# Cosine attention: the four transfers of the inverse norms divided between SyncE and ScalarE

## The reference

```python
def _L1_attn_ref(x, w_q, w_kv, w_out, b_out, scale):
    ...
    q = _l2norm(q) * jnp.exp(scale)
    k = _l2norm(k)
    sim = jnp.einsum('bhid,bhjd->bhij', q, k)
    attn = jax.nn.softmax(sim, axis=-1)
    out = jnp.einsum('bhij,bhjd->bhid', attn, v)
    out = out.transpose(0, 2, 1, 3).reshape(b, s, h * out.shape[-1])
    return out @ w_out + b_out
```

## Time and profile before

| | |
|---|---|
| median of 3 runs | 6519.71 us (6516.19 to 6521.88) |
| the profiled execution's own time | 6522.74 us |
| its span, first to last instruction | 6520.8 us |
| busy TensorE | 5878.9 us, 90% of the span |
| busy VectorE | 4384.8 us, 67% |
| busy ScalarE | 3402.6 us, 52% |
| busy GpSimd | 2289.2 us, 35% |
| transfers of the inverse norms (`cosine_inv_all`) | 256, all issued by SP, 128 KB each |
| transfers of the inverse denominators (`cosine_rden`) | 256, all issued by SP, 64 KB each |

### The profile page before, as it was taken

The page is one execution under the profiler, slowest core; times in us unless marked ns, Lnnn a source line. Parts: engine busy times, 40 slices in busy tenths (PEclk is TensorE's granted clock), DMA queues, the critical chain, the costliest instruction groups (busy, mean ns, idle before and its releaser), DMA issues.

```text
span 6520.8 us, 129965 instructions
## 1 busy us (share of the span) xinstructions
PE 5878.9 (90%) x51681; PEld 3219.8 (49%) x51681; DVE 4384.8 (67%) x7178; ACT 3402.6 (52%) x5560; POOL 2289.2 (35%) x1597
## 2 busy tenths in 40 slices
PE   7999878999677778998689999999999999999998
PEld 3555554444422225765445555555555555555554
DVE  4656434454288894334678888888878788887885
ACT  3444324656144443444456656666666666665664
POOL 0111101222034441000055555555555555555553
PEclk9999978999688888998799999999999999999998
DMA  5555302333100000000011111111111111111110
GB/s 138 115 115 119 89 0 53 80 82 83 44 3 0 0 0 1 1 0 1 24 36 32 40 43 34 31 47 37 34 45 38 33 44 40 34 39 41 38 37 24
DMA packets 298945, 275.95 MB, mean 42 GB/s; under 512 B 40580, under 2 KB 289572, under 8 KB 298148
## 3 DMA queue, kind: packets, MB, share of 16 engines
q1 hardware_dynamic: 298372, 268.00, 17.7%
HBM read 30.88 MB, written 2.10 MB: 5 GB/s over the span
## 4 chain that ended last, share of the span: by engine, by line
PE 33%; issue 5%; DVE 5%; POOL 5%; ACT 2%; DMA 0%; POOLq 0%; DVEq 0%; SPq 0%; ACTq 0%
PE banks L2254 7%; PE banks L2289 6%; PE banks L2324 5%; PE banks L2309 4%; PE banks L2267 3%; PE banks L2341 3%; DVE local_probs L2559 2%; POOL local_rot L2653 2%; POOL local_ssum L2645 2%; PE banks L2363 2%; PE banks L2313 2%; PE banks L2274 1%; ACT local_probs L2455 1%; DVE local_gate L2584 1%; DVE local_sin L2540 1%
## 5 line engine op out<-in xcount | busy, mean ns | idle before, releaser
L2645 POOL TENSOR_TENSOR local_ssum<-local_sq 128x512 f32<-128x512 f32 x384 | 697.5, 1816 | 2145.1 <-ACT local_sq L2433 2144.6
L2653 POOL TENSOR_TENSOR local_rot<-local_rot,local_inv_all 128x512 f32<-128x512 f32 x768 | 964.6, 1288 | 94.1 <-DMA local_inv_all<-local_inv 93.6
L2254 PE MATMUL banks<-local_y,local_Wqkv 128*128 128x512 f32 x1536 | 823.0, 618 | 64.0 <-ACT local_sq L2433 61.2
L2559 DVE TENSOR_TENSOR local_probs<-banks,band 128x576 f32<-128x576 f32 x768 | 546.2, 753 | 185.4 <-PE banks L2289 180.1
L2455 ACT ACTIVATE local_probs<-local_probs,local_npeak 128x1152 f32<-128x1152 f32 x384 | 482.8, 1257 | 357.1 <-DVE local_probs L2559 357.1
L2539 DVE TENSOR_TENSOR local_rot<-banks,local_rotary_scaled 128x512 f32<-128x512 f32 x768 | 525.6, 684 | 191.1 <-PE banks L2254 185.6
L2433 ACT ACTIVATE local_sq<-banks 128x512 f32<-128x512 f32 x768 | 459.4, 598 | 253.6 <-DVE local_sin L2540 244.8
L2546 DVE TENSOR_TENSOR local_rot<-local_rot,local_sin 128x1024 f32<-128x1024 f32 x384 | 513.7, 1338 | 41.9 <-DVE local_sin L2540 2.3
L2449 ACT COPY local_v<-banks 128x512 f32<-128x512 f32 x384 | 224.9, 586 | 594.1 <-PE banks L2267 593.6
L2289 PEld LDWEIGHTS banks<-local_rot 32*128 32x128 f32 x12288 | 416.7, 186 | 225.0 <-issue 200.8
L2540 DVE TENSOR_TENSOR local_sin<-banks,local_rotary_scaled 128x512 f32<-128x512 f32 x768 | 522.4, 680 | 0.0
(11 more groups left out here) (400 smaller groups left out, 10561.4 us busy)
## 6 DMA issues: line engine op xcount, KB each, us to landing
local_inv_all<-local_inv SPq DMA_DIRECT2D x768, 128.0 KB, 2.7
favor_half_norm_all<-favor_half_norm SPq DMA_DIRECT2D x512, 128.0 KB, 3.0
cosine_inv_all<-cosine_inv SPq DMA_DIRECT2D x256, 128.0 KB, 2.6
favor_rden<-favor_inv SPq DMA_DIRECT2D x256, 64.0 KB, 2.1
cosine_rden<-cosine_inv_den SPq DMA_DIRECT2D x256, 64.0 KB, 2.1
local_Wqkv<-in_L_ffn_Wqkv_quads SPq DMA_DIRECT2D x36, 256.0 KB, 2.9
local_Wo<-in_L_ffn_Wo_quads SPq DMA_DIRECT2D x6, 512.0 KB, 4.1
experts_w_W<-in_L_ffn_W SPq DMA_DIRECT2D x1, 2048.0 KB
```

Source lines behind the costliest of these rows:

```text
L2254: pe.matmul(seqs(banks[:, QK_BANK, :]), Wqkv[:, at:at + P], y_group(g), start=True, stop=True).then_inc(qk_projected, 1)
L2559: dve.tensor_tensor(probs[:, e % 3, r:r + 2, :], banks[:, S_BANK + r:S_BANK + r + 2, 0:SCORES], consts["band"].unsqueeze(1).broadcast_to([ ...
L2645: pool.tensor_tensor(ssum[:, n % 2, m, :], sq[:, 0, :], sq[:, 1, :], ALU.add).then_inc(square_summed, 1)
L2653: pool.tensor_tensor(a, a, twice(inv_all[:, n % 2, m, of_seq(s)]), ALU.mult).then_inc(united, 1)
```

## The change

SP's `send_inverse` issues two transfers (c = 0 and 1, q's) in place of four. ScalarE, right behind the Exp that makes the inverse norms, waits for that Exp's own signal (`inverted`) and for the reading of the buffer two units before (`unit`), and issues the other two (k's). The source's form is the same and now comes from a helper, `spread_rows`. The semaphores and the counts that the others wait for are unchanged.

```diff
--- before.py
+++ after.py
@@ -726,6 +726,10 @@
         tiles = lambda g: x[:, g * GT:(g + 1) * GT, :]
         of_seq = lambda s: slice(s * SEQ, (s + 1) * SEQ)
 
+        def spread_rows(n, c):
+            rows_c = inv[32 * c:32 * c + 32, n % 2, :]
+            return bass.AP(rows_c.tensor, rows_c.offset, [rows_c.ap[0], [0, 4], rows_c.ap[-1]])
+
         with nc.Block() as block:
             @block.sync
             def _(sp):
@@ -733,10 +737,8 @@
                     sp.wait_ge(inverted, n + 1)
                     if n >= 2:
                         sp.wait_ge(unit, 2 * n - 2)
-                    for c in range(4):
-                        rows_c = inv[32 * c:32 * c + 32, n % 2, :]
-                        source = bass.AP(rows_c.tensor, rows_c.offset, [rows_c.ap[0], [0, 4], rows_c.ap[-1]])
-                        sp.dma_start(inv_all[:, n % 2, c // 2, of_seq(c % 2)], source).then_inc(inv_sent[n % 2], 16)
+                    for c in range(2):
+                        sp.dma_start(inv_all[:, n % 2, 0, of_seq(c)], spread_rows(n, c)).then_inc(inv_sent[n % 2], 16)
 
                 def send_den(n):
                     sp.wait_ge(den_inverted, n + 1)
@@ -899,6 +901,11 @@
                     if n == 0:
                         act.wait_ge(up_ready, 1)
                     act.activation(inv[:, n % 2, :], ss[:, n % 2, :], ACT.Exp, bias=up[:], scale=-0.5).then_inc(inverted, 1)
+                    act.wait_ge(inverted, n + 1)
+                    if n >= 2:
+                        act.wait_ge(unit, 2 * n - 2)
+                    for c in range(2):
+                        act.dma_start(inv_all[:, n % 2, 1, of_seq(c)], spread_rows(n, 2 + c)).then_inc(inv_sent[n % 2], 16)
 
                 def copy_v(n):
                     g, t, half = group_of(n), pair_of(n) % GT, pair_of(n) // GT
```

## The result

The changed kernel takes 6599.4 us (median of 4 runs, 6593.3 to 6603.8) against 6518.0 us of the kernel before in the same comparison: the ratio is 1.0122, with a 95% interval of 1.0107 to 1.0137. That is 79 us slower by the ratio (81 by the two medians). The forecast was 6566 us, slower by 46.7 us, with a range from 6506 to 6642. The sign, the place and the range hold; the size is 33 us short.

What follows compares the result with a forecast made beforehand. Bound: the cosine stage's ring through late transfers and `unite`, TensorE in output steps. Afterwards ScalarE's copy of v: -41.5 + 63 x 1.40 = +46.7 us on 6519.7 gives 6566 us, range 6506 to 6642.

Steps and rivals of the forecast that it cites:

- The ring: Cosine attention stage: clamp, ScalarE's Ln and Exp, SP's four issues, `unite`, q's copy, next clamp; TensorE outside without output projection.
- what is late next: ScalarE's copy of v, then k's projection and TensorE's work behind it; a plain step becomes 7.98 us + d.
- The normalising step: Step without output that normalises x: VectorE held 1.10 us, half covered, estimated 8.45 us without d.
- d: Hold-up of ScalarE's next activation by the wait and two issues, per step; taken as 1.40 us.
- The sum: Stage's 63 steps, 28 with output and 35 without: 566.0 us + 63 d against 607.5, +46.7 us.
- step 2: ScalarE gets a wait and two issues: 0.10 + 1.21 + 0.09 = 1.40 us a step; nothing hides it.
- The clock: TensorE's granted clock: 87% busy after the change, expected to stay at the 2.4 GHz level, effect nothing.
- case B: The two queues take turns, ScalarE held for all four issues: d = 2.6, +122 us, 6642 us; chance 0.15.
- A: Issues overlap and cost ScalarE what they cost SP: d 0.9 to 2.0, +15 to +84 us; chance 0.62.
- Rival D: Cheap issue, d below 0.45, leaves ScalarE's order free; `unite` gains, at most 27 us faster, 6493 us; chance 0.10.
- TensorE's own time: Floor for steps without output: 8.21 us plain, about 8.45 on average; steps with output stay at 10.10.
- Rival E: GpSimd's sum gets between `unite`'s two operations; q's copy waits 0.45 us longer in 35 steps, +16 us atop A.

Runs made afterwards that it cites:

- the variant behind the copy of v: Changed kernel with ScalarE's two issues moved behind its copy of v; ratio 0.9969 to the kernel before.
- the faster versions: Issues behind the copy of v 0.9969, behind the exps 0.9972; kernel before with separate q and k semaphores 0.9963, both edits 0.9957, k's transfers left out 0.9965.

## Why the prediction was right, and where it was short

*The ring and what is late next:* right. By the clamp's starts the steps of the change are 9.80 us plain (7.98 + 1.82 = 9.80), 11.59 with output (9.79 + 1.82 = 11.61), 12.20 with output and the statistics (10.38 + 1.82 = 12.20):

```profile
1432.29 0.41 DVE L991 TENSOR_SCALAR cosine_ss<-banks 128x256 f32<-128x256 f32 x1
...
1443.88 0.42 DVE L991 TENSOR_SCALAR cosine_ss<-banks 128x256 f32<-128x256 f32 x1
...
1456.08 0.41 DVE L991 TENSOR_SCALAR cosine_ss<-banks 128x256 f32<-128x256 f32 x1
```

*The normalising step:* 8.45 was an estimate, with d it gives 10.27 us; it is 10.65 (1456.08 to 1466.73), and 11.45 in three of the six such steps. The four operations on x take 1.61 us here, beside GpSimd's sum, in place of 1.10: the collision that `unite` avoids has moved on to them.

```profile
1463.79 1.57 POOL L1038 TENSOR_TENSOR cosine_summed<-cosine_probs 128x512 f32<-128x512 f32 x1 [1.79 <-ACT cosine_probs L926]
...
1464.59 1.61 DVE L978 TENSOR_SCALAR cosine_xn<-x,cosine_moments,cosine_rstd 128x128 f32<-128x128 f32 x4 [0.36 <-ACT cosine_rstd L880]
```

*The sum:* 566 + 63 x 1.82 = 680.7 us against 682.5 measured. What failed is one term, in step 2: d was 0.10 + 1.21 + 0.09 = 1.40, and is 1.82. By the rows above the wait's 0.10 is 0.13 (the issue starts at 1468.16 where the exp would have at 1468.03), the restart's 0.09 is 0.13 (1469.72 to 1469.85), and the two issues are 1.56 instead of 1.21. 63 x 0.42 = 26.5 us of the 28.3 by which the stage's growth of 75.0 exceeds the 46.7; that the ratio gives some 4 us more than the profiled executions, and the medians 6, no run here explains.

*The clock:* the prediction put it at nothing. In four steps of the stage it was granted at 0.85, and these are longer: three normalising steps, 11.45 us where the others with a clock of 1.00 are 10.65, and one other, 11.44 us (1112.92 to 1124.36) where its like are 9.81. That is 4.0 us together, and the normalising steps are 0.4 us longer than estimated even at 1.00. That the ring comes out within 1.8 us all the same is in part luck: it spreads the 35 steps without output evenly over four kinds, 8.75 of each, where the trace has six normalising ones, and this errs the other way.

*Why the issues were mis-sized:* I took SP's price, with the argument that it is the same transfer. It is, and alone ScalarE pays the same (1.21 us for two). What I left out is what SP's two beside them do to it. I had that as case B, all or nothing, +122 us, with a chance of 0.15. The truth lies between A and B: the first issues overlap nearly in full, the second of ScalarE is some 0.3 us longer. The Trainium skill (Perfetto Trace Analysis, DMA Instruction — HWDGE) says that the descriptor generator is locked for exclusive use and that the wait for the lock is in the profiled time. By that rule ScalarE's second issue would hold such a wait. The trace agrees only in that an issue gets longer. The two first issues run side by side for nearly their whole 0.59 and 0.56 us, and in the variant behind the copy of v the second takes 0.91 us when SP's issues are over (1452.37 against 1452.45), so a wait for a generator that SP holds isn't shown. What lengthens the second issue stays open.

*Rival D (faster if the issue is cheap):* its limit, TensorE's own time, is what the faster versions run into. I had its condition as a cheap issue only. The other way to it, an issue of the same price at a place where ScalarE has activations in hand, wasn't among the cases: "nothing hides it" in step 2 is right for the place chosen, not for ScalarE's issues as such.

*Rival E (GpSimd wins the race):* not in the rows above. Both operations of `unite` are done in 1.28 us, GpSimd's sum starts 0.83 us behind the first and reads 1.56 us where it was 1.27, so it is the sum that gets longer. Over the stage the operations of `unite` take 0.72 us on average, where they took 1.13 before.

## What to carry to other kernels

In this kernel a transfer issued by ScalarE cost the issue's whole length for everything queued behind it where it stood behind a wait for ScalarE's own last result: 1.82 us for two issues, with the wait; the same two a few independent instructions later ran mostly beside them and held the copy of v up by 0.46 us. So before an issue is moved off a queue, ask what is queued behind the new place and which instruction the engine could still be working on. And before work is divided between queues, see whether the consumer needs all of it at once: here a semaphore for each half gained 24 us with no second queue at all.

## What the runs showed of the hardware

- With SP issuing none of them, an issue of this transfer took ScalarE 0.62 or 0.63 us by the median, and SP 0.605. With both queues issuing pairs, ScalarE's first took 0.59 us and its second 0.95, and SP's pair kept its 1.20 us. The second took 0.91 us also where SP's pair had ended 0.08 us before it started.
- ScalarE's issues start while earlier activations are still running: one started 0.50 us ahead of an activation that precedes it in the program (1451.87 and 1452.37), with no wait on that activation between.
- TensorE's granted clock was 0.91 on average over 500 us where its weight load waited 2.9 us a step for the copy of v, and 0.99 where it waited 1.9 us. A step with the same 72 matmuls took 12.56 us at a granted clock of 1.00 and 14.20 us at 0.88.
